# Reordering the last thirteen steps of an attention turn: transposes, then scores, then all fill in one run

## The reference, cut to what matters

```python
q = q * cos + _rotate_half(q) * sin
scores = jnp.einsum('bhqd,bhkd->bhqk', q, k) * scale
scores = jnp.where(causal[None, None], scores, jnp.asarray(-1000000000.0, dt))
attn = jax.nn.softmax(scores, axis=-1)
out = jnp.einsum('bhqk,bhkd->bhqd', attn, v)
return out @ Wo.T
```

## Time and profile before

| | |
|---|---|
| median of 3 runs | 2385.06 us (2380.48 to 2385.91) |
| the profiled execution, own time | 2382.02 us |
| its span, first to last instruction | 2380.2 us |
| TensorE (PE) busy | 2369.0 us |
| ScalarE (ACT) busy | 1621.9 us |
| VectorE (DVE) busy | 1430.2 us |
| GpSimd (POOL) busy | 579.8 us |

### The profile page before, as it was taken

One profiled execution on the slowest core, in us unless ns is written; L12 is line 12 of the kernel. 1 busy time (PEld: TensorE's weight loads), 2 busy tenths in 40 slices (PEclk: granted clock), 3 DMA queues, 4 the chain that ended last, 5 costly groups with the idle time before them and its releaser, 6 DMA issues.

```text
span 2380.2 us, 41136 instructions
## 1 busy us (share of the span) xinstructions
PE 2369.0 (100%) x12028; PEld 1993.7 (84%) x12028; DVE 1430.2 (60%) x3796; ACT 1621.9 (68%) x3224; POOL 579.8 (24%) x453
## 2 busy tenths in 40 slices
PE   9999999999999999999999999999999999999998
PEld 7888888888888888888888888888888888888887
DVE  5334666666767676766667676766676675242333
ACT  4223878788888888887878888887888885222221
POOL 3002323233332423232323333232323220000000
PEclk9999999999999999999999999999999999999999
DMA  7867444444353444344444445354444345420110
GB/s 272 303 214 290 131 147 138 132 137 149 137 172 106 171 140 146 128 145 139 135 140 141 142 132 164 118 172 123 160 135 145 129 138 194 140 71 36 53 36 18
DMA packets 133271, 340.24 MB, mean 143 GB/s; under 512 B 13344, under 2 KB 30752, under 8 KB 122656
## 3 DMA queue, kind: packets, MB, share of 16 engines
q1 hardware_dynamic: 133216, 339.53, 42.3%
HBM read 232.00 MB, written 111.67 MB: 144 GB/s over the span
## 4 chain that ended last, share of the span: by engine, by line
PE 96%; issue 1%; DVE 1%; ACT 1%; DMA 1%; SPq 0%; POOL 0%; POOLq 0%; DVEq 0%
PE b_ps L267 45%; PE b_sps L267 34%; PE b_tps L1571 10%; PE b_tps L1630 3%; PE b_ps L1630 3%; PE b_tps L267 1%; DMA a_raw<-in_wkrT 0%; PE b_sps L1580 0%; DMA b_kt<-k_d 0%; ACT b_pt L1068 0%; ACT b_sc L1053 0%; ACT b_sc L1047 0%; DVE b_sc L1272 0%; DVE a_xs L1196 0%; POOL a_wkr L930 0%
## 5 line engine op out<-in xcount | busy, mean ns | idle before, releaser
L1290 DVE TENSOR_TENSOR b_pt<-b_tps,b_pt 128x512 fp32r<-128x512 f32 (+3 forms) x768 | 426.7, 556 | 301.5 <-ACT b_pt L1068 297.2
L267 PE MATMUL b_sps<-b_kt,b_qs 128*128 128x512 f32 (+4 forms) x2304 | 497.1, 343 | 0.2 <-DMA b_kt<-k_d 0.2
L1053 ACT ACTIVATE b_sc<-b_sc,b_rinv 128x896 f32<-128x896 f32 (+7 forms) x512 | 396.1, 774 | 105.4 <-DVE b_rinv L1280 98.8
L267 PEld LDWEIGHTS b_sps<-b_kt,b_qs 128*128 128x128 f32 x2304 | 403.2, 188 | 55.6 <-issue 0.9
L1068 ACT ACTIVATE b_pt<-b_tps 128x512 fp32r<-128x512 f32 (+3 forms) x768 | 367.6, 479 | 115.7 <-PE b_tps L1571 113.9
L267 PE MATMUL b_ps<-b_xs,b_wq 128*128 128x512 f32 x1536 | 440.7, 406 | 0.0
L267 PE MATMUL b_ps<-b_pt,b_vt 128*128 128x512 f32 x1584 | 435.9, 402 | 0.3 <-DVE b_ys L1301 0.3
L267 PE MATMUL b_ps<-b_wo,b_ot 128*128 128x512 f32 x1536 | 423.9, 405 | 0.1
L1047 ACT ACTIVATE b_sc<-b_sc,b_nmax 128x896 f32<-128x896 f32 (+7 forms) x512 | 395.4, 772 | 40.1 <-DVE b_nmax L1272 37.0
L1272 DVE CUSTOM_DVE_ANT_0 b_sc<-b_sps,b_mask 128x896 f32<-128x896 f32 (+7 forms) x512 | 386.5, 755 | 16.2 <-PE b_sps L267 16.1
L1571 PE MATMUL b_tps<-b_ident,b_sc 128*128 128x128 f32 x2304 | 374.3, 272 | 1.4 <-DVE b_pt L1290 1.3
(11 more groups left out here) (142 smaller groups left out, 2274.5 us busy)
## 6 DMA issues: line engine op xcount, KB each, us to landing
b_xs<-xs_d SPq DMA_DIRECT2D x32, 2048.0 KB, 9.0
b_ys<-y_d SPq DMA_DIRECT2D x128, 256.0 KB, 2.7
y_d<-b_ys SPq DMA_DIRECT2D x128, 256.0 KB, 3.0
k_d<-a_ks SPq DMA_DIRECT2D x32, 512.0 KB, 3.9
v_d<-a_vs SPq DMA_DIRECT2D x32, 512.0 KB, 3.0
b_kt<-k_d SPq DMA_DIRECT2D x64, 256.0 KB, 4.3
b_vt<-v_d SPq DMA_DIRECT2D x16, 1024.0 KB, 4.8
b_wraw<-in_wqT SPq DMA_DIRECT2D x64, 256.0 KB, 2.8
```

The lines of the kernel that those rows point to most:

```text
L267: ins = nc.tensor.matmul(out, *every[n], start=(n == 0), stop=(n == len(every) - 1))
L1053: nc.scalar.activation(sc[:, slot, 0:w], sc[:, slot, 0:w], ACT.Copy, scale=rinv[:, slot:slot + 1])\
L1290: nc.vector.tensor_tensor(pt[:, u, LO, 0:nj, h * P:(h + 1) * P], tps[n % 2][:, 0:nj], pt[:, u, HI, 0:nj, h * P:(h + 1) * P], ALU.subtract) ...
```

## The change: what it does

In steps 19 to 31 of every turn that has cells there, each engine gets a new order. TensorE: both groups of transposes first, then the scores, then the fill of the step in one run; before it was scores, fill, group 0, fill, group 1, fill. ScalarE: "take", the rounding of group 0 and group 1, then normalise, exp, weights, q; before it was take, normalise, group 0, exp, weights, group 1, q. VectorE: reciprocal, take, the subtraction of both groups, the maximum, q; before, the maximum stood ahead of both groups. The GpSimd and DMA lists stay, and so do the number of instructions and which fill matmuls belong to which step.

```diff
 SHARES = ((1,), (0, 1), (1, 1.25, 1))
+FRONT = 19
+ACT_FRONT = ("take", 0, 1, "normalise", "exp", "weights", "q")
+DVE_FRONT = ("take", 0, 1, "max", "q")
+PE_FRONT = (0, 1, "scores", "fill")
...
                 for step in steps_of(turn):
-                    for job in ACT_ORDER[part_of(step)]:
+                    for job in ACT_FRONT if step >= FRONT else ACT_ORDER[part_of(step)]:
...
-                    for job in DVE_ORDER[part_of(step)]:
+                    for job in DVE_FRONT if step >= FRONT else DVE_ORDER[part_of(step)]:
...
-                    shares = cut(parts, SHARES[len(ts)])
-                    for job in (0, 1, "scores") if step == 0 else PE_ORDER[part_of(step)]:
+                    shares = cut(parts, (1,) if step >= FRONT else SHARES[len(ts)])
+                    order = PE_FRONT if step >= FRONT else PE_ORDER[part_of(step)]
+                    for job in (0, 1, "scores") if step == 0 else order:
```

## The result

| | before | after |
|---|---|---|
| median | 2383.75 us | 2443.93 us (2441.55 to 2448.84) |
| ratio, 95% interval | | 1.0257 [1.0242, 1.0272] |
| span of the profiled execution | 2380.2 us | 2442.2 us |
| a turn of the loop, first scores to first scores, mean of 14 | 111.03 us | 114.84 us |
| last turn, first scores to last scores | 92.5 us | 95.7 us |

The turns are measured in the timeline of TensorE. Turns 0 to 14 together grew by 56.8 us. To its last scores the last turn grew by 3.2, but 0.9 of that is only that these scores now stand behind eight transposes; to the first matmul of stage C it grew by 2.8 (from 107.6 to 110.4).

A forecast was written before the change was run, and what follows sets the result against it. TensorE was taken as the bound, busy 2369.0 of 2380.2 us. Waits of 2.72 us in 15 turns (40.8) plus 3 in the last gave 44 us, so 2382 became 2426 and the median 2429; range 2406 to 2450.

The forecast's parts named there:

- TensorE's own work: Steps 19 to 31: one change fewer between transposes and products per step, gain 0 to 2 us, taken as 0.
- The waits in a turn: TensorE waits for late normalises at steps 21, 27, 29 and for banks in 24, 28: 2.72 us a turn.
- the q bank of step 24: Step 24: the second q job waits 0.26 us for its bank, behind two swaps and cos_q.
- step 28's bank: Step 28: pv 5 waits 0.31 us for its bank, behind weights, hi_q, swaps and cos_q.
- the 0.04 in step 28: A further TensorE wait of 0.04 us in step 28, counted in the turn's sum.
- the loop sum: Rounding 0 to end of exp at width 896: 0.63 + 0.61 + 0.34 + 1.12 + 1.05 = 3.75 us.
- The last turn: Short steps, nearly each from 22 on waiting 0.1 to 0.9 us: 4.1 less some 1, taken as +3 us.
- What was to show it: Some 45 transpose waits for normalise, 0.5 to 0.8 us; none for subtractions; busy sums within some us; wrong if for a DMA.
- A: Bank waits and step 21's wait vanish, those of steps 27 and 29 remain: 26 us, 2411; chance 0.15.
- B: Cascade: hi_q and add_q late too, bank waits grow, steps 25, 28, 30 wait too: 75 us, 2460; chance 0.12.
- C: Not slower: every normalise still in time before the next step's transposes, 2383 to 2385 us; chance 0.08.
- D: Transpose runs lower TensorE's clock to 1.2 GHz in scores and some fill: 270 us, 2700; chance 0.01.

The follow-up runs named there:

- e4: Changed kernel, but scores precede both transpose groups on TensorE, normalise precedes both roundings on ScalarE, maximum precedes both subtractions on VectorE; 2379.65 us, ratio 0.9981.
- e10: e4 unchanged, run once more beside e9 on one chip; 2381.10 us, ratio 0.9988 to the kernel before.
- e7: e4 with TensorE back in the order before (scores, fill, group 0, fill, group 1, fill); 2381.72 us, ratio 0.9993 to the kernel before.
- e9: e4 with a share of fill between single transposes in steps 19 to 31, as far as fill goes; 2391.76 us, ratio 1.0038 to the kernel before.
- e1: Changed kernel, but in step 31 the scores stand ahead of both groups of transposes; 2427.40 us, ratio 1.0181 to the kernel before.
- e5: e1 with GpSimd instead of ScalarE rounding the prepared feed-forward weights in steps 24 and 27; 2413.96 us, ratio 1.0132 to the kernel before.
- e3: Changed kernel with TensorE in the new order, but ScalarE and VectorE in the old one; 2545.54 us, ratio 1.0678 to the kernel before.

## Why the prediction was right, and what it missed

The forecast was 2429, slower, with 0.92 on that side, and its mechanism is what happened. Measured is 2443.93, inside the range of 2406 to 2450, but the loss of 60 us is over a third above the 44 us of the forecast. That it lies inside is in part luck: the range had room above for ScalarE's timing and for a cascade, and what filled it was neither.

**TensorE's own work.** Taken as 0, bounds 0 and 2 us of gain. e4 and e10 against e7 give 1.4 and 0.9 us in turns 1 to 14, e9 confirms the sign. Right.

**The waits in a turn.** Forecast at step 21, the q bank of step 24, step 27, step 28's bank and step 29: 0.63, 0.26, 0.68, 0.31, 0.80. Turn 7 shows 0.55, 0.47, 0.66, 0.35, 0.85. The sum was 2.72 with the 0.04 in step 28, and is 2.88. With the key wait removed (e1), a turn is 2.95 us longer than before. One term of the loop sum, 1.12 us for the maximum, is in none of the prediction's rows (1.01 from start to start); after the change, exp starts 1.13 us after the maximum does (1113.59 and 1112.46).

**The last turn.** Forecast 3, measured 2.8 to the start of stage C.

**The step that failed** is the one that isn't there: the prediction lists what the moved transposes wait for and what waits for them, but for the scores, which moved behind them, it names no DMA. Their end is what releases the key loads, and 7.4 us of TensorE work behind them just covered those loads, whose last landed 7.0 to 7.4 us behind them; the prediction even reckoned step 0's 21 fill matmuls, and did not ask what they hide. The missing term is 0.9 us a turn by the prediction's own 0.11 a transpose, 11.5 us in the list of waits and 13 us with turn 0 in e1's turns. With it the forecast would have been 2442.

**What was to show it.** Waits at steps 21, 27 and 29 and for banks are there. The view names VectorE's L1294 for 31 of 50 where I had said ScalarE's L1057, and had said that waits for L1294 would go. The start times and e5 say that ScalarE's work is what was late. The busy sums did not stay within some us: TensorE's rose by 21.0 and VectorE's fell by 21.8. The point that it would be wrong if the waits were for a DMA came in part true.

**The rivals.** A, only some of the waits: out, all five are there. B, a cascade: out; steps 25 and 30 lost under 0.03 us against e10 in the mean of turns 1 to 14, step 28 about what was forecast (0.38 for 0.35), and the excess has another cause. C, not slower: out. D, the clock: out; with all transposes in runs of five to eight the granted clock was at its 2.4 GHz level in every slice, 0.999 in the mean.

## What to carry to other kernels

When an order is turned on an engine that never waits, write down for every moved instruction what its end releases, the DMAs first, and how much work lies between that and its user: here the covers of the normalise, of two PSUM banks and of the key loads were each short by less than a microsecond, and that was nearly the whole loss. The order on a producing engine and those on its consumers are one design; here each half alone cost two to three times what both cost together (130 and 162 us for 60). And the instruction that is late is not always the one to move: one that fills a wait elsewhere in the loop is better left there.

## What the runs showed of the hardware

Going from transposes to fp32 products and back cost TensorE 0.005 to 0.013 us (e4 and e10 against e7, e9 against e10), far less than one of its waits.

How late a transpose started after what it had waited for depended on which wait it was. In turns 1 to 14 it was 0.13 us after ScalarE's normalise (42 cases in the changed kernel) and 0.06 us after VectorE's subtraction (167 cases in e3). In the last turn of e3 it was 0.15 after the subtraction, as in the earlier trace rows. Why it differs no run here shows.

The wait list counted 41 us where the turns show 60, because up to 0.27 us of a wait lie under the modelled end of the matmul ahead (0.40 in the list and 0.66 by the starts, at step 27).
